# Attention and a gated feed-forward layer on one core: one PSUM bank moved from the row maxima to the scores

## The reference

```
q, k, v = x @ w.T + b, split into 16 heads of 8
scores  = einsum("bhqd,bhkd->bhqk", q, k) / sqrt(16)
out     = einsum("bhqk,bhkd->bhqd", softmax(scores), v)
x       = layernorm(x + out @ wo.T + bo)
h       = silu(x @ w1.T * s1) * (x @ w2.T * s2)
h       = gelu(h @ h1.T * s); h = gelu(h @ h2.T * s)
x       = layernorm(x + h @ w3.T * s3)
```

## Time and profile before

| | |
|---|---|
| time, median of 3 runs (lowest, highest) | 443.16 us (442.76, 443.18) |
| profiled execution: span from first to last instruction | 441.5 us |
| TensorE busy | 427.8 us, 97% |
| VectorE busy | 386.5 us, 88% |
| ScalarE busy | 367.7 us, 83% |
| GpSimd busy | 90.3 us, 20% |
| granted TensorE clock | 1.000 over the whole span (2.4 GHz) |

### The profile page before, as it was taken

The page is one execution under the profiler, slowest core; times in us unless marked ns, Lnnn a source line. Parts: engine busy times, 40 slices in busy tenths (PEclk is TensorE's granted clock), DMA queues, the critical chain, the costliest instruction groups (busy, mean ns, idle before and its releaser), DMA issues.

```text
span 441.5 us, 9824 instructions
## 1 busy us (share of the span) xinstructions
PE 427.8 (97%) x3496; PEld 227.0 (51%) x3498; DVE 386.5 (88%) x719; ACT 367.7 (83%) x694; POOL 90.3 (20%) x142
## 2 busy tenths in 40 slices
PE   8999999999999999999999999999899899999995
PEld 4543544444444444444444443544333488877884
DVE  6799999999999999999999999999884577657636
ACT  4487989998998999989899899999899886678762
POOL 9730000100000010000001002373311263046103
PEclk9999999999999999999999999999999999999999
DMA  6567741111130110113011001021021000000101
GB/s 165 176 196 129 270 147 33 44 28 28 48 122 25 45 31 28 27 48 122 25 46 33 26 27 49 14 43 47 15 39 50 13 8 1 1 2 2 48 1 48
DMA packets 17117, 24.88 MB, mean 56 GB/s; under 512 B 5169, under 2 KB 9009, under 8 KB 16689
## 3 DMA queue, kind: packets, MB, share of 16 engines
q1 hardware_dynamic: 16464, 23.68, 19.3%
q10 hardware_dynamic: 608, 0.59, 0.5%
HBM read 15.08 MB, written 7.60 MB: 51 GB/s over the span
## 4 chain that ended last, share of the span: by engine, by line
PE 76%; DVE 10%; ACT 5%; SPq 3%; DMA 2%; issue 2%; POOL 0%; POOLq 0%; DVEq 0%; ACTq 0%
PE ps L1369 24%; PE ps L1291 20%; PE ps L1479 16%; DVE negmax L977 9%; PE ps L1353 8%; ACT arena L664 2%; DMA parts_q<-arena 2%; PE ps L1223 2%; PE ps L1234 1%; PE ps L1423 1%; PE ps L1319 1%; PE ps L1263 1%; SPq L463 1%; SPq L435 1%; ACT v_pad L722 1%
## 5 line engine op out<-in xcount | busy, mean ns | idle before, releaser
L977 DVE TENSOR_REDUCE negmax<-ps 128x1 f32<-128x512 f32 x458 | 275.8, 701 | 1.8 <-PE ps L1291 1.5
L664 ACT ACTIVATE arena<-ps 128x512 f32<-128x512 f32 x360 | 190.0, 606 | 19.3 <-PE ps L1353 14.1
L1353 PE MATMUL ps<-qx,kx 64*128 64x512 f32 x512 | 171.3, 451 | 0.9 <-DMA qx<-mT 0.6
L1291 PE MATMUL ps<-kx,qx 61*128 61x512 f32 x468 | 160.2, 441 | 0.6 <-DMA qx<-parts_q 0.5
L1291 PEld LDWEIGHTS ps<-kx,qx 61*128 61x128 f32 x468 | 75.1, 184 | 88.6 <-DVE negmax L977 79.3
L1369 PE MATMUL ps<-arena,v_pad 128*32 128x256 f32 (+3 forms) x1328 | 104.8, 407 | 2.8 <-ACT arena L664 2.8
L664 ACT ACTIVATE hf<-ps 128x512 f32<-128x512 f32 x152 | 83.2, 604 | 9.4 <-PE ps L1353 8.4
L1353 PEld LDWEIGHTS ps<-qx,kx 64*128 64x128 f32 x512 | 78.9, 184 | 18.6 <-ACT arena L664 11.8
L1479 PE MATMUL ps<-hid,w_high 128*128 128x512 f32 (+1 forms) x296 | 68.3, 388 | 0.8 <-issue 0.4
L1479 PEld LDWEIGHTS ps<-hid,w_high 128*128 128x128 f32 x296 | 54.2, 188 | 12.3 <-issue 0.8
L1369 PEld LDWEIGHTS ps<-arena,v_pad 128*32 128x32 f32 x1328 | 28.5, 108 | 37.1 <-issue 30.7
(11 more groups left out here) (107 smaller groups left out, 317.2 us busy)
## 6 DMA issues: line engine op xcount, KB each, us to landing
qx<-parts_q SPq DMA_DIRECT2D x60, 64.0 KB, 2.1
late_sb<-in_late SPq DMA_DIRECT2D x3, 1280.0 KB, 5.5
kx<-parts_k SPq DMA_DIRECT2D x56, 64.0 KB, 2.2
parts_q<-prt SPq DMA_DIRECT2D x3, 512.0 KB, 6.4
parts_q<-arena SPq DMA_DIRECT2D x3, 512.0 KB, 8.3
xT_sb<-in_xT SPq DMA_DIRECT2D x4, 256.0 KB, 4.2
xT_sb<-arena SPq DMA_DIRECT2D x28, 32.0 KB
prt<-den SPq DMA_DIRECT2D x7, 128.0 KB
```

The lines of the kernel that those rows point to most:

```text
L664: nc.scalar.activation(probs(n // HG)[:, heads(n), :], ps[:, PLAN["score", n][0], :], ACT.Exp, scale=SCALE).then_inc(exp_done, 1)
L977: nc.vector.tensor_reduce(negmax[:, t // TURNS % 2, m % 2, h * QT + q:h * QT + q + 1], ps[:, MAX_BANK + m % 4, :], AX.X, ALU.max, negate=T ...
L1291: nc.tensor.matmul(ps[:, half_bank(m), :], qx[at, slot, qc, h, q * P:(q + 1) * P], kx[at, slot, h, part * C:(part + 1) * C], start=True, s ...
L1353: nc.tensor.matmul(ps[:, bank, :], kx[at, slot, h % PAIR, kt * P:(kt + 1) * P], qx[at, slot, qc, h % PAIR, :], start=True, stop=True)\
```

## The change

Three things change together.

- Banks: the loop's halves take the three banks 4, 2, 3 in turn (`LOOP_BANKS`, `loop_bank`), so half m waits for reduction m - 3 (`pe.wait_ge(max_taken, m + 1 - 3)`). Bank 5 goes into the rotation of the scores, which has four banks beside the held one; a score waits for the exponential of four scores before. `LATE_BANKS` is bank 4 alone. The number of score banks after the last half is five, as before.
- The start of the loop: the last tiles ahead of the loop still use banks 2 to 5. `LEFT_BY` says for each bank which count of reductions frees it, and the first three halves and the first score in bank 5 wait for it.
- VectorE's loop is written out: every reduction waits for a constant, and there is no register work and no branch.

The order of TensorE's and ScalarE's instructions is the same.

```
-FIRST_BANKS, LATE_BANKS = [7, 0, 6, 1], (4, 5)
+FIRST_BANKS, LATE_BANKS = [7, 0, 6, 5, 1], (4,)
 MAX_BANK = 2
+LOOP_BANKS = (4, 2, 3)
...
+LEFT_BY = {fold_bank(t): 2 * (t + 1) for t in range(WHOLE)}
+def loop_bank(m):
+    return LOOP_BANKS[(m - 2 * WHOLE) % len(LOOP_BANKS)]
 def bank_plan():
-    order, last, plan = FIRST_BANKS[:-1], {}, {}
+    order, plan = FIRST_BANKS[:-1], {}
+    last = {bank: ("reduced", LEFT_BY[bank]) for bank in order if bank in LEFT_BY}
...
 def half_bank(m):
-    return MAX_BANK + (m + 2 * (FOLD // 2 + 1) if m < 2 * FOLD else m) % 4
+    return MAX_BANK + (m + 2 * (FOLD // 2 + 1)) % 4 if m < 2 * FOLD else loop_bank(m)
...
-            def turn_half(i, m):
-                dve.wait_ge(max_scores, i * (2 * PER * TURNS) + m + 1)
+            def turn_half(m):
+                dve.wait_ge(max_scores, m + 1)
...
-            with dve.Fori(0, ITERS - 1) as i:
-                turn_halves_from(i, 2 * WHOLE, 2 * WHOLE + 2 * PER * TURNS)
...
-            turn_halves_from(ITERS - 1, 2 * WHOLE, 2 * WHOLE + 4 * KT)
+            at_invert = 2 * ((ITERS - 1) * PER * TURNS + WHOLE) + 4 * KT
+            turn_halves_of(2 * WHOLE, at_invert)
             invert(0)
-            turn_halves_from(ITERS - 1, 2 * WHOLE + 4 * KT, 2 * PER * TURNS)
-            larger(ITERS - 1, PER - 1)
+            turn_halves_of(at_invert, 2 * U_ALL * TURNS)
+            larger(U_ALL - 1)
...
-                if 2 * WHOLE <= m < 2 * WHOLE + 4:
-                    pe.wait_ge(max_taken, 2 * (m - WHOLE - 3))
+                if 2 * WHOLE <= m < 2 * WHOLE + len(LOOP_BANKS):
+                    pe.wait_ge(max_taken, LEFT_BY[loop_bank(m)])
+                elif m >= 2 * WHOLE:
+                    pe.wait_ge(max_taken, m + 1 - len(LOOP_BANKS))
                 elif m >= 4:
                     pe.wait_ge(max_taken, m - 3)
```

More of the change, by code:

```diff
@@ L124, in unit_to, with fold_bank @@
     return next((k // KT for k, _, c1 in pieces_of(g) if c1 == C and k % KT == KT - 1), None)
+def fold_bank(t):
+    return MAX_BANK + (t + WHOLE) % 4
+LEFT_BY = {fold_bank(t): 2 * (t + 1) for t in range(WHOLE)}
+def loop_bank(m):
+    return LOOP_BANKS[(m - 2 * WHOLE) % len(LOOP_BANKS)]
 def bank_plan():
-    order, last, plan = FIRST_BANKS[:-1], {}, {}
+    order, plan = FIRST_BANKS[:-1], {}
+    last = {bank: ("reduced", LEFT_BY[bank]) for bank in order if bank in LEFT_BY}
     held = FIRST_BANKS[-1]
@@ L198, in head_of @@
     return 2 * (t % 2) + t % TURNS // (2 * QT), t % TURNS // 2 % QT
-def fold_bank(t):
-    return MAX_BANK + (t + WHOLE) % 4
 def apart_bank(t):
@@ L970, in turn_folded, with larger @@
                   .then_inc(max_taken, 2)
-            def turn_half(i, m):
-                dve.wait_ge(max_scores, i * (2 * PER * TURNS) + m + 1)
+            def turn_half(m):
+                dve.wait_ge(max_scores, m + 1)
                 t = m // 2
-                h, q = head_of(t % (PER * TURNS) + PER * TURNS)
+                h, q = head_of(t)
                 nc.vector.tensor_reduce(negmax[:, t // TURNS % 2, m % 2, h * QT + q:h * QT + q + 1],
-                                        ps[:, MAX_BANK + m % 4, :], AX.X, ALU.max, negate=True)\
+                                        ps[:, loop_bank(m), :], AX.X, ALU.max, negate=True)\
                   .then_inc(max_taken, 1)
-            def larger(i, w):
-                dve.wait_ge(max_taken, i * (2 * PER * TURNS) + (w + 1) * 2 * TURNS)
+            def larger(w):
+                dve.wait_ge(max_taken, (w + 1) * 2 * TURNS)
                 if w > 0:
-                    dve.wait_ge(max_split, i * PER + w)
+                    dve.wait_ge(max_split, w)
                 nc.vector.tensor_tensor(negmin[:, w % 2, :], negmax[:, w % 2, 0, :], negmax[:, w % 2, 1, :],
@@ L997, in _, with turn_halves_of @@
             dve.wait_ge(max_split, 1)
-            def turn_halves_from(i, m0, m1):
+            def turn_halves_of(m0, m1):
                 for m in range(m0, m1):
-                    turn_half(i, m)
+                    turn_half(m)
                     if m % (2 * TURNS) == 0:
-                        larger(i, m // (2 * TURNS) - 1)
-            with dve.Fori(0, ITERS - 1) as i:
-                turn_halves_from(i, 2 * WHOLE, 2 * WHOLE + 2 * PER * TURNS)
+                        larger(m // (2 * TURNS) - 1)
             def invert(n):
```

## The result

| | before | after |
|---|---|---|
| median of the runs (lowest, highest) | 443.08 us (442.76, 443.18; 4 runs) | 451.81 us (451.39, 452.18; 4 runs) |
| ratio, 95% interval | | 1.0197 (1.0185 to 1.021) |
| profiled execution: span | 441.5 us | 449.9 us |
| last reduction starts at | 314.2 us | 322.8 us |
| from there to the end of the span | 127.3 us | 127.1 us |

The change costs 8.7 us; 452.3 was predicted, within 448.6 to 455.2. All of the loss is in the attention loop: behind the last reduction the two profiled executions are equally long.

What follows compares the result with a forecast made beforehand. VectorE was taken to bound the attention loop at 0.598 us a reduction. Third maximum bank 7.6, transposes 2.1 and fourth score bank -0.6 sum to +9.1 us: 443.16 + 9.1 = 452.3 us, range 448.6 to 455.2.

Steps and rivals of the forecast that it cites:

- VectorE bounds the loop before, and TensorE's lead of four halves covers the products: Attention loop before: VectorE needs 1.794 us a group, TensorE 1.68, running up to four halves ahead.
- The ring of 3.70 us for two groups: Round of waits over TensorE's products and VectorE's reductions: 1.848 us a group against 1.794, 7.6 us over 141 groups.
- Transposes at 0.16 each, 2.1 us: TensorE, between products and next group's first half: once a unit, 13 times from 58 us; lower bound 1.4.
- The fourth score bank, -0.6: Scores' loads on TensorE: removes up to 21 waits of 11.8 us, but only 0.6 us gained where VectorE waited.
- The spread of the reduction's duration: VectorE's reduction, median 703 ns, nearer 0.72 us where ScalarE is dense; 0.02 us makes 1.4 us in all.
- Written-out loop, 0: VectorE's loop: removing register instructions and round ends is worth 0, since register work lies beside the reduction before.
- Start of the loop and what is behind it, 0: Some tenths of a us at the start, absorbed by DMA rows at 42.9 us; the rest moves as a whole.
- What the profile would show: Loop: VectorE near 100% busy, five distances 0.598 and one 0.71, some 322 reductions, last near 323.5, scores' waits one or two.
- every group pays: Rival: the third half's delay of 0.11 us comes in each group, not each second: 460 us; chance 0.06.
- TensorE does not pay for the wait at c: Rival: 1.11 us from third half to next group's first, 1.80 a group, loss 2.4 us: 445.6; chance 0.07.
- no change: Rival: VectorE keeps its pace, as a freed bank and TensorE's spare 0.11 us a group suffice: 443.0; chance 0.04.
- faster: Rival: the fourth score bank gives VectorE halves sooner than the third maximum bank takes them away: 442.3; chance 0.04.

Runs made afterwards that it cites:

- a longer stretch: Kernel with three maximum and three score banks, plus one 128-column matmul on TensorE behind each group's products: 465.41 us, ratio 1.0507.
- The disturbance repeated by itself: Kernel with three maximum and three score banks, plus one small matmul behind the products only once a unit: 456.82 us, ratio 1.0314.
- the three-and-four kernel: Changed kernel (three maximum, four score banks) with VectorE's loop again a hardware loop with registers, two rounds of 192 halves: 454.09 us, ratio 1.0247.

## Why the prediction was right

- *VectorE bounds the loop before, and TensorE's lead of four halves covers the products.* Right: with four banks the distance is 0.598 whichever way VectorE's loop is written.
- *The ring of 3.70 us for two groups.* Right, 3.69 measured; the runs with two banks, with two score banks, with moved products and with a longer stretch all follow the same sum with other terms. The price of the third bank alone, without the fourth score bank, was larger than the 7.6 + 2.1 I gave: 12.0. What I had not counted are the late products at the changes of a unit. They are there in the kernel before as well (c is loaded at 99.26, its products at 100.12, 0.86 us later), but five reductions from 99.70 take 3.09 us and so stand 0.60 apart: VectorE's backlog hid them as it did the transposes. The halves left at 58 us are 425 by the trace and not 422, which is nothing in the sum.
- *Transposes at 0.16 each, 2.1 us.* In the changed kernel the reductions' distance at a transpose is 0.83 to 0.86 us in two units of three and 0.75 in the third, where the ring alone gives 0.69: on the mean 0.12 each, 1.6 for 13. The disturbance repeated by itself gave 0.12 each too. That lies between my two bounds, 1.4 and 2.1, and I had taken the upper one.
- *The fourth score bank, -0.6.* This step was mis-sized: -3.3. I took the 11.8 us of waits in the earlier trace rows as spread over the loop. In the window of 60 to 314 us of the same trace they are 0.5:

```profile
PEld ps L1353 <- ACT arena L664: 0.5, 2, 0.3
```

The rest stands before 60 us and behind the last half. What the fourth bank is worth could not be read there: it takes away the late products at a unit's change, mostly 0.2 to 0.34 us each beyond the usual 0.43, which cost something only once the third maximum bank is gone. So I left the same thing out twice, as a cost of the third bank (12.0 in place of 9.7) and as a gain of the fourth score bank (3.3 in place of 0.6), and the change makes both moves at once. That these two errors cancel, and the total is good to 0.4 us, is luck as far as my reasoning goes.

- *The spread of the reduction's duration.* I wrote that it is nearer 0.72 where ScalarE is dense. The trace does not bear that out: its median is 720 ns from 180 to 220 us, where ScalarE is busy 90%, and 684 from 280 to 300, where it is busy 97%. The changed kernel's is 682 throughout.
- *Written-out loop, 0.* Right with four banks (1.0005). But my reason was half of it. I set the rule on taken branches of the Trainium skill ("Runtime: NRT & Kernel Launch", "Instruction fetch mechanics") aside, since nothing is seen at the branch of a round of 128 halves. With a round of 192 halves the loop costs 2.0 us more than the written-out one, and its trace has 2.2 us at the taken branch. The trace of that run agrees with the rule in what it shows, a stall of 3.3 us behind the branch with a packet of instructions in it; that the target lay outside of the fetched window is not shown. The shorter round is free of it.
- *Start of the loop and what is behind it, 0.* Behind the loop right (127.3 and 127.1 us). And near 58 us nothing has been lost, as written: the 34th reduction starts at 58.08 us before and at 58.13 after. Before, VectorE stands idle there for 0.50 us; after, it does not, since the slower loop has used that time up. Other executions differ here by more (57.2 us in the run with VectorE's loop written out, 59.7 in the changed kernel's second one), so this agreement to 0.05 us is partly chance.
- *What the profile would show.* Right on the busy share, the two-group pattern and the count (322 said, 323 found), the last reduction near 323.5 (322.8); wrong on the scores' waits for ScalarE, which fell from 11.8 us to 9.0 only.

The rivals: "every group pays" and "TensorE does not pay for the wait at c" are out by the length of 3.69 (they would have some 3.8 and 3.60), "no change" and "faster" by the result.

## What to carry to other kernels

When two engines hand tiles to each other through n buffers, follow the wait round: the producer's stretch without tiles, the hand-over, the consumer's run to the buffer that is waited for, the release. Divide by the groups it spans and hold it against each engine's own pace; a buffer can be given away as long as that sum is the smaller one, and how busy the engines look does not tell. Delays that a backlog hides before the change (here transposes and late products) enter the sum once the backlog is gone, so look for them too. An engine whose instructions overlap in the rows can lose 3% of its pace at a busy share of 99%, so count its instructions in a fixed window.

## What was not expected of the hardware

A hardware loop's end on VectorE is free with 128 reductions in a round (next register instruction 0.35 and 0.32 us after the two taken branches, beside a running reduction). With 192 in a round the one taken branch is followed by 3.3 us without an instruction of the sequencer and costs 2.2 us. That is one branch in one trace; where between the two lengths it begins is open.

The rows of the same reduction have a median of 703 ns in the kernel before and 677 in the one with constants and the same banks. The register instructions are not the cause by themselves, since with them the three-and-four kernel reads 681. In the kernel before it is a drift: 680 ns at 40 to 60 us, 720 at 180 to 220, while the distances stay at 0.598. What it is stays open.
